# One kernel, one change: where the queue of loads puts the third quad's expert weights

## What is computed

```python
x = x + attention(layernorm_over_channels(x))            # (8, 64, 256), 32 key/query channels
t = to_tokens(x)                                         # 2048 tokens of 64 channels
flat = layernorm(t)
probs = softmax(flat @ router_w.T)                       # 8 experts
topk_probs, topk_idx = top_k(probs, 2)                   # normalised to sum 1
h = silu(flat @ w1[e].T) * (flat @ w3[e].T)              # hidden 682, for each chosen expert e
y = h @ w2[e].T
out = t + sum over the 2 chosen experts of gate * y
```

## Time and profile before

| what | us |
|---|---|
| median of 3 runs | 174.97 |
| lowest, highest | 174.4, 175.56 |
| profiled execution | 175.2 |
| its span in the profile | 173.1 |
| TensorE busy with products | 144.0 (83%) |
| GpSimd busy | 85.7 (50%) |
| VectorE busy | 97.8 (57%) |
| ScalarE busy | 71.5 (41%) |

### The profile page before, as it was taken

How to read it: one execution, slowest core, us unless ns; L and a number is a source line. 1 busy time by engine, 2 the same in 40 slices (tenths; PEclk the granted TensorE clock), 3 DMA queues, 4 the chain that set the end, 5 groups by cost and what they waited for, 6 DMA issues and landing times.

```text
span 173.1 us, 4872 instructions
## 1 busy us (share of the span) xinstructions
PE 144.0 (83%) x1682; PEld 120.4 (70%) x1682; DVE 97.8 (57%) x364; ACT 71.5 (41%) x141; POOL 85.7 (50%) x114
## 2 busy tenths in 40 slices
PE   0669949578788699899699999999999999984782
PEld 0446737367277279797598989899999999874262
DVE  0645695785762888769554646455555736443050
ACT  2148666241144037253363636363545454542011
POOL 2685427887771477777071625344343526356000
PEclk9999997955555579999999999999999999999698
DMA  4999400100882492279896979596969981010434
GB/s 117 326 287 296 107 0 15 31 19 27 238 340 55 106 399 110 58 193 397 249 370 189 378 226 376 168 398 159 386 174 366 278 326 38 5 31 15 113 137 121
DMA packets 19892, 32.99 MB, mean 191 GB/s; under 512 B 7691, under 2 KB 13100, under 8 KB 19868
## 3 DMA queue, kind: packets, MB, share of 16 engines
q1 hardware_dynamic: 16732, 29.55, 52.6%
q0 software_dynamic: 2272, 2.35, 4.2%
q10 hardware_dynamic: 864, 0.79, 1.5%
HBM read 25.55 MB, written 7.13 MB: 189 GB/s over the span
## 4 chain that ended last, share of the span: by engine, by line
issue 30%; POOL 26%; PE 22%; DVE 9%; DMA 5%; ACT 5%; POOLq 1%; SPq 0%; DVEq 0%; ACTq 0%
POOL ys L366 20%; PE psum L927 7%; POOL xs L357 5%; PE psum L916 4%; PE psum L896 3%; ACT xn L422 2%; DMA y_in<-ys 2%; PE psum L1105 2%; PE psum L887 2%; DMA proj<-projections 1%; PE psum L882 1%; DMA ys<-y_out,y_row 1%; DVE parts L620 1%; ACT probsT L456 1%; DVE rows L591 1%
## 5 line engine op out<-in xcount | busy, mean ns | idle before, releaser
L366 POOL DMA_INDIRECT ys<-y_out,y_row x39 | 37.4, 958 | 45.3 <-DVE y_out L839 36.2
L1033 PE MATMUL psum<-x_cols,weights 64*128 64x128 f32 x390 | 49.5, 279 | 1.6 <-DMA weights<-experts 1.2
L1035 PE MATMUL psum<-x_cols,weights 64*128 64x128 f32 x390 | 49.7, 279 | 0.0
L1033 PEld LDWEIGHTS psum<-x_cols,weights 64*128 64x128 f32 x390 | 45.6, 188 | 5.7 <-issue 3.8
L827 DVE TENSOR_TENSOR hid<-psum,act_sb 128x512 f32<-128x512 f32 (+1 forms) x50 | 33.8, 677 | 23.4 <-ACT act_sb L500 23.1
L1035 PEld LDWEIGHTS psum<-x_cols,weights 64*128 64x128 f32 x390 | 45.7, 188 | 0.0
L500 ACT ACTIVATE act_sb<-psum 128x512 f32<-128x512 f32 (+1 forms) x50 | 29.3, 587 | 25.2 <-PE psum L1033 24.7
L357 POOL DMA_INDIRECT xs<-xrows,pos x32 | 31.6, 988 | 11.6 <-issue 8.6
L1061 PE MATMUL psum<-hid,weights 128*64 128x128 f32 x468 | 28.8, 276 | 0.2 <-DVE hid L827 0.2
L1061 PEld LDWEIGHTS psum<-hid,weights 128*64 128x64 f32 x468 | 25.9, 137 | 2.0 <-DVE hid L827 0.4
L927 PEld LDWEIGHTS psum<-u_sb,probsT 128*128 128x128 f32 x64 | 11.3, 266 | 5.2 <-ACT probsT L456 2.8
(11 more groups left out here) (147 smaller groups left out, 178.4 us busy)
## 6 DMA issues: line engine op xcount, KB each, us to landing
weights<-experts SPq DMA_DIRECT2D x39, 565.0 KB, 4.8
xs<-zeros SPq DMA_DIRECT2D x4, 1040.0 KB, 11.9
x_in<-xs SPq DMA_DIRECT2D x39, 32.5 KB
ys<-y_out,y_row POOLq DMA_INDIRECT x39
xs<-xrows,pos POOLq DMA_INDIRECT x32, 2.3
y_in<-ys ACTq DMA_DIRECT2D x2, 256.0 KB, 4.6
y_in<-ys SPq DMA_DIRECT2D x2, 256.0 KB, 4.4
x_sb<-x_tok SPq DMA_DIRECT2D x1, 384.0 KB, 3.8
```

The source lines that it names most:

```text
L366: nc.gpsimd.indirect_dma_start(ys, bass.IndirectOffsetOnAxis(ap=y_row[:, j:j + 1], axis=0), y_out[:, i % RING, h, :], None).then_inc(y_sca ...
L1033: first_ = nc.tensor.matmul(H1_BANK[g % 2][:, src], weights[0:C, slot, P * s:P * (s + 1)], x_cols[0:C, i % 2, src], start=True, stop=True)
L1035: second_ = nc.tensor.matmul(H3_BANK[g % 3][:, src], weights[C:P, slot, P * s:P * (s + 1)], x_cols[C:P, i % 2, src], start=True, stop=True)
```

## The change

Three edits, all in the order of instructions.

- The owners of a phase get a semaphore of their own, `owners_ready`, which the last instruction of `owners_of_slots` raises (before, that instruction raised VectorE's step counter, and only `table_ready` told SyncE).
- SyncE waits for `owners_ready` of the first phase, and then reads one owner and issues its weights' DMA, four times; then it waits for `table_ready`. In the second phase it waits for `owners_ready`, reads the owners of quad 2 and issues its weights, and only then waits for `table_ready`, reads the rows' numbers, waits for the landed rows and loads them. From the third phase on the order of loads is the old one, with one more wait in front.
- GpSimd sends the third pair's eight scatters without a break, and does the fourth pair's `t_deviation` behind them instead of after the second.

```diff
--- before.py
+++ after.py
@@ -188,7 +188,7 @@
         dispatched = [sem(f"dispatched{p}") for p in range(PHASES)]
         variance_t_ready, rstd_t_ready = sem("variance_t_ready"), sem("rstd_t_ready")
         shifted, exponents, gates_ready = sem("shifted"), sem("exponents"), sem("gates_ready")
-        keep_ready, table_ready = sem("keep_ready"), sem("table_ready")
+        keep_ready, owners_ready, table_ready = sem("keep_ready"), sem("owners_ready"), sem("table_ready")
 
         w_loaded = [sem(f"w_loaded{i}") for i in range(WSLOTS)]
         x_in_loaded = [sem(f"x_in_loaded{i}") for i in range(XRING)]
@@ -295,21 +295,29 @@
             def landed(p):
                 sp.wait_ge(dispatched[p], 16 * TPP * K_TOP * (KNOWN[p] - (KNOWN[p - 1] if p else 0)))
 
+            sp.wait_ge(owners_ready, 1)
+            for h in members(0):
+                owner = sp.value_load(table[0:1, 0, h:h + 1], min_val=0, max_val=E - 1)
+                sp.dma_start(weights[:, h, :], experts[bass.ds(owner, 1)].rearrange("o p c -> p (o c)")).then_inc(w_loaded[h], 16)
             sp.wait_ge(table_ready, 1)
-            load_weights(0, owners_of(0))
             early_rows, second_owners = [rows_of(0), rows_of(1)], owners_of(1)
             landed(0)
             load_rows(0, early_rows[0])
             load_rows(1, early_rows[1])
             load_weights(1, second_owners)
             for p in range(1, PHASES):
+                sp.wait_ge(owners_ready, p + 1)
+                opening = quads_of(p)[0]
+                if opening < WQUADS:
+                    load_weights(opening, owners_of(opening))
                 sp.wait_ge(table_ready, p + 1)
                 for i in quads_of(p):
                     at = rows_of(i)
-                    if i == quads_of(p)[0]:
+                    if i == opening:
                         landed(p)
                     load_rows(i, at)
-                    load_weights(i, owners_of(i))
+                    if i >= WQUADS:
+                        load_weights(i, owners_of(i))
 
             all_scattered(sp)
             for q in range(0, QUARTERS, 2):
@@ -404,11 +412,11 @@
             t_deviation(0)
             for p in range(PAIRS):
                 for at in range(TPP * K_TOP):
-                    if p == 0 and at == TPP * K_TOP - 2 or p == 2 and at == K_TOP:
-                        t_deviation(p + 1)
+                    if p == 0 and at == TPP * K_TOP - 2:
+                        t_deviation(1)
                     scatter_row(p, at)
-                if p == 1:
-                    t_deviation(2)
+                if 1 <= p < PAIRS - 1:
+                    t_deviation(p + 1)
             for j in range(NS):
                 scatter_result(j)
 
@@ -675,8 +683,7 @@
                 chain(nc.vector.tensor_tensor(passed[:, own, :], slot_at[:, own].unsqueeze(2).to_broadcast([P, n, E - 1]),
                                               ends[:, 1:E].unsqueeze(1).to_broadcast([P, n, E - 1]), ALU.is_ge))
                 with nc.allow_low_precision(reason="numbers of experts: whole and below 2^3"):
-                    nc.vector.tensor_reduce(table[:, 0, own], passed[:, own, :], AX.X, ALU.add).then_inc(dve_step, 1)
-                steps[0] += 1
+                    nc.vector.tensor_reduce(table[:, 0, own], passed[:, own, :], AX.X, ALU.add).then_inc(owners_ready, 1)
 
             def jumps_between_owners(p):
                 if p == 0:
```

## The result

| | us |
|---|---|
| median after (4 runs, 177.9 to 181.85) | 179.93 |
| median before beside them (4 runs, 174.4 to 175.56) | 175.2 |
| ratio, with its 95% interval | 1.021 [1.013, 1.028] |
| profiled execution after | 178.78, span 176.9 |

The account below looks back on a forecast made before the run. TensorE, hardly resting from the first quad's products, was taken as the bound. Late rows +3.0, weights' wait -1.21, third quad -0.45 and next three -0.57 made +0.8 on 174.97: 175.8 us, range 173.4 to 177.5.

Parts of the forecast that it names:

- SyncE as a plain sequence: SyncE's queue has no slack: four table reads cost 2.40 us, one quad about 8.9 us, so lateness is never made up.
- the third pair's scatters in one go: GpSimd's eight scatters run from 50.08 to near 60.1, 7 us earlier; the 2.3 us wait for landed rows goes.
- the last deviation hidden: GpSimd's last deviation begins near 60.2 instead of 58.17; VectorE's steps hide it with over 2.5 us in hand.
- the weights' wait gone: TensorE's 1.21 us wait for the third quad's weights goes, since they land before 75.
- 0.15 us left of the third quad's 0.68: Third quad on TensorE: of the 0.68 us lost there about 0.2 stays, counted as -0.45.
- the next three quads at 26.91: TensorE's three quads after the third lose their 0.57 us, as SyncE runs about 3 us ahead.
- the first quad's order worth nothing: First quad's weights issued one by one, about 0.8 us earlier, but wanted only after 62: worth 0.
- The pairing: Third quad's rows paired at 75.9, 10.9 us after the first weight issue, 3.0 us later than before (1.2 to 3.4).
- Rival (a): Third quad's row loads don't queue behind the weights: pairing at 74.1, -1.0 us, 174.0; chance 0.25.
- (b): Rows don't queue behind weights, and VectorE's hold-up in the second quad goes too: -1.8 us, 173.2; chance 0.1.
- the clock full from the sixteenth slice on: Reading of the earlier profile page: TensorE's granted clock half from the ninth to fourteenth slice, full from the sixteenth.
- rival (c): TensorE's 3.85 us rest in the second quad halves its clock, costing 1.7 us: +2.5, 177.5; chance 0.2.

Follow-up runs that it names:

- the second trace: The changed kernel run once more, unchanged, for another profile: 178.29 us, ratio 1.012 to the kernel before.
- the tiny loads: Changed kernel with four 8-column loads where the third quad's weights stood, and those weights behind its rows: 175.94 us, ratio 0.998 to the kernel before.
- two fills: Kernel with the third quad's weights back behind its rows, plus two useless VectorE fills ahead of that quad's pairing: 177.34 us, ratio 1.000 to the kernel before.
- with three: Kernel with the third quad's weights back behind its rows, plus three useless VectorE fills ahead of that quad's pairing: 177.58 us, ratio 1.008 to the kernel before.
- rows first: Changed kernel with the third quad's weights put back behind its rows, all else as changed: 173.33 us, ratio 0.988 to the kernel before.

## Why the prediction was wrong

**Right**, and seen as written: SyncE as a plain sequence (owners complete to first weight issue 2.39 us, forecast 2.4; to the row loads 6.7, forecast near 7.2); the third pair's scatters in one go and the last deviation hidden (VectorE asked for it at 65.2, it was there by 62.0); the weights' wait gone; 0.15 us left of the third quad's 0.68, forecast 0.2; the next three quads at 26.91; the first quad's order worth nothing. The pairing came 11.1 us after the first weight issue, and 12.1 in the second trace, forecast 10.9 with a bound of 11. Rival (a), that the rows don't queue behind the weights, and (b) with it, fall by the tiny loads: the traffic costs 1.5 to 2.5. One reading was not right: the forecast called the clock full from the sixteenth slice on, but slices 38 and 40 of the earlier trace rows show 6 and 8.

**Wrong** was that the sum behind 175.8 put the clock at nothing. It stood only in rival (c), "TensorE's wait drops its clock ... It decides from a gap near 3.5 us", with a chance of 0.2 against 0.45 for the forecast without it. The clock fell in both traces of the changed kernel, 1.8 and 1.9 us into gaps of 3.01 and 3.89, and cost 2.1 and 2.0 us. I had one gap of 3.52 us with a fall behind it and waits of 1.21 and less without, and put the point of decision at the far end of what lay between. The length of the gap alone doesn't decide it: gaps of 1.64 and 1.88 us left the clock alone and one of 2.06 did not, but three of 3.52 left it alone too. My own sum had a gap of 3.85, above even my bound, so (c) should have been the likeliest case. Its price was well sized: 1.7 forecast, 2.0 to 2.1 measured.

Rival (c) had +2.5 us in all. The traces have +2.9 and +3.7 from the owners to the seventh quad, the ratios +3.6 and +2.1. Without the clock's part the traces leave 0.8 and 1.7 us, where the forecast had 0.8: in the first trace the rest of the sum holds; in the second the rows were paired 1 us later after the owners, and why stays open.

That the measured 179.93 and 178.29 are above even 177.5 is in part a spread that I took for smaller than it is. Three runs of the kernel before gave a narrow picture: beside the later kernels the same kernel had medians of 175.8 to 176.8, and runs from 173.5 to 181.5. The traces show where some of it arises, in all kernels alike. The first product comes between 61.9 and 64.3 us. TensorE's clock is half then in twelve of the thirteen traces and rises 0.2 to 2.9 us later: where it rises at once the first quad takes 9.0 or 9.1 us (six traces, with the one where the clock was full already), where it rises late 10.1 or 10.2 (six traces), and once 9.5. It took 10.16 with two fills and 9.08 with three, two kernels that are alike up to there. And from the seventh quad's first product to the end the traces took 52.7 to 54.5 us; the longest are the three in which the clock fell only behind the second of the late rests, and that with rows first (54.4).

**The better version** is the change without its main edit: GpSimd's scatters in one go, rows ahead of weights, 0.987 and 0.988 of the kernel before.

## What to carry to other kernels

A transfer issued ahead of its need is free only if nothing more urgent stands behind it on the same queue or moves beside it (here the rows' loads and the rows' scatter): write down what the issuing engine does next, with the price of each read and issue, and when that is wanted. When a sum lengthens a wait of TensorE while its clock is full, price the clock as well as the wait; here rests from 2.06 us on mostly brought a fall, though three of 3.52 did not, and a few products of no use in the gap kept the clock. And undo edits one at a time: here one edit of three was worth -1.3% and another cost 3%.

## What the runs showed of the hardware

In the second quad the granted clock fell to half at rests of 2.06, 3.01, 3.07, 3.89 and 3.91 us: 1.8 or 1.9 us into the rest in four of them, and only at the end of that of 3.07. It stayed full over 1.64 us, and over 1.88 that followed 2.1 us of products. I had expected some 3.5. At the late rest of 3.52 us it fell in ten traces and stayed full in three. Half clock then lasted 3.4 us or 6.8. The Trainium skill ("TensorE: Matmul & The Clock Gate", Why this matters for your kernels) says to avoid longer rests of TensorE between bursts, since the clock drops. The traces agree with the direction, but not with the length that the page warns of: there are falls at shorter rests (2.06 us) and three longer ones without a fall (3.52 us), so here the measurement decides. A scatter of 128 rows, sent while four weight loads were moving, was in 5.4 us after GpSimd was done with it instead of 1.4, by the end of SyncE's wait for it.
